# Shorter windows for the indirect transfers of a graph network kernel: scatters four deep, gathers of edge features six deep

## What is computed

```
h = relu(layernorm(x));  x += gated_network(h)   # 4 steps: msgs = (h W_k + b_k)[etype, src]; a = segment_sum(msgs, dst); GRU
h = relu(layernorm(x));  x += attention(h)       # softmax over the edges of a source, sum at the target
h = relu(layernorm(x));  x += segment_sum(h[src], dst)
h = relu(layernorm(x));  x += MLP(sum, max, mean of edge_attr over the edges of each src)
```

## Time and profile before

| | us |
|---|---|
| runs | 8828.69, 8854.78, 8858.06 |
| median | 8854.78 |
| profiled execution | 8876.89 |
| its span | 8875.0 |

### The profile page before, as it was taken

The page is one execution under the profiler, slowest core; times in us unless marked ns, Lnnn a source line. Parts: engine busy times, 40 slices in busy tenths (PEclk is TensorE's granted clock), DMA queues, the critical chain, the costliest instruction groups (busy, mean ns, idle before and its releaser), DMA issues. The chain is left out here.

```text
span 8875.0 us, 66244 instructions
## 1 busy us (share of the span) xinstructions
PE 4613.8 (52%) x21729; PEld 2818.2 (32%) x21729; DVE 4824.9 (54%) x9853; ACT 4454.6 (50%) x2943; POOL 3692.8 (42%) x3327
## 2 busy tenths in 40 slices
PE   0110001311113777676385555757839668788866
PEld 0100001100001333333274444546728556211135
DVE  9963346200002777776374333745629446888863
ACT  0000000200002999997385445647929668688855
POOL 0067773677775000000467444274865753000041
PEclk9555555555555888888697777878969879555578
DMA  9710000300101777777296555767829656455566
GB/s 415 340 0 0 0 0 29 94 18 7 33 4 64 298 303 297 303 296 266 90 310 182 150 165 167 231 182 243 307 74 343 222 201 235 177 223 219 217 241 217
DMA packets 523231, 1589.94 MB, mean 179 GB/s; under 512 B 148178, under 2 KB 207929, under 8 KB 493190
## 3 DMA queue, kind: packets, MB, share of 16 engines
q1 hardware_dynamic: 329082, 1408.51, 44.1%
q10 hardware_dynamic: 88332, 146.04, 5.0%
q0 software_dynamic: 105472, 31.16, 2.7%
HBM read 1046.14 MB, written 539.23 MB: 179 GB/s over the span
## 5 line engine op out<-in xcount | busy, mean ns | idle before, releaser
L1016 ACT ACTIVATE full<-ring 128x3136 fp32r<-128x3136 uint8 x731 | 1995.9, 2818 | 793.8 <-remote 469.6
L858 PE MATMUL ps_all<-full,TR 128*128 128x448 f32 x8232 | 1864.9, 383 | 651.1 <-ACT full L1016 248.0
L623 POOL DMA_INDIRECT mat_d<-cT,idxT x1563 | 1660.2, 1062 | 945.0 <-issue 485.2
L666 POOL DMA_INDIRECT two<-in_edge_attr,eid x1029 | 1183.2, 1150 | 1858.4 <-DMA csum_d<-two 1379.0
L858 PEld LDWEIGHTS ps_all<-full,TR 128*128 128x128 f32 x8232 | 1583.3, 196 | 929.5 <-issue 463.1
L809 PE MATMUL ps_all<-ring,T 128*64 128x448 f16 x8232 | 1159.5, 408 | 1377.3 <-issue 993.6
L1030 ACT ACTIVATE ring<-ring 128x3136 uint16<-128x3136 uint8 x197 | 553.4, 2809 | 1268.6 <-remote 1141.5
L809 PEld LDWEIGHTS ps_all<-ring,T 128*64 128x64 bf16 x8232 | 556.0, 124 | 1979.1 <-issue 1409.8
L1469 DVE CAST full<-ring 128x1568 fp32r<-128x1568 uint8 x487 | 478.5, 983 | 966.6 <-remote 451.9
L761 PE MATMUL ps_all<-ident,two 128*128 128x128 f32 x448 | 109.1, 424 | 1275.2 <-DVE two L1174 1113.2
L666 POOL DMA_INDIRECT ring<-in_edge_attr,eid x539 | 608.5, 1129 | 164.3 <-issue 164.3
(11 more groups left out here) (419 smaller groups left out, 6139.2 us busy)
## 6 DMA issues: line engine op xcount, KB each, us to landing
ring<-mat_d SPq DMA_DIRECT2D x784, 784.0 KB
mat_d<-ring SPq DMA_DIRECT2D x98, 1568.0 KB, 39.8
csum_d<-two SPq DMA_DIRECT2D x192, 784.0 KB
two<-csum_d SPq DMA_DIRECT2D x32, 3136.0 KB, 10.2
base_d<-two SPq DMA_DIRECT2D x49, 1568.0 KB
TR<-two_d SPq DMA_DIRECT2D x282, 256.0 KB
C<-csum_d SPq DMA_DIRECT2D x17, 3136.0 KB, 10.2
C<-base_d SPq DMA_DIRECT2D x49, 800.0 KB
```

The source lines that it names most:

```text
L623: pool.indirect_dma_start(mat_d, bass.IndirectOffsetOnAxis(idxT[:, col:col + 1], 0), cT[:, col:col + 1], None).then_inc(s_sc[g % 8], 16)
L666: pool.indirect_dma_start(slab[n % SLABS][:, c, 0:FA], None, attr, bass.IndirectOffsetOnAxis(eid[:, at:at + 1], 0)).then_inc(s_at[n % SLAB ...
L858: mm = pe.matmul(accs[:, j, 0:GW], parts.bitcast(F32R), full[:, m % WIDES, j * GW:(j + 1) * GW].bitcast(F32R), start=first, stop=True, ski ...
L1016: act.activation(to, own, ACT.Copy).then_inc(s_ha, 1)
```

## The change

`FETCHES = 6` and `AFLOAT = 4` are new. The scatters count on 4 semaphores in turn, one for each scatter instead of one for each group, and scatter k waits until scatter k - 4 has landed. `s_done` is raised ahead of the fifth scatter of the next group instead of the ninth. Gather `at` counts on semaphore `at % 6` and waits until gather `at - 6` has landed, across the slabs. VectorE waits for all six semaphores ahead of a scan.

```diff
+FETCHES = 6
+AFLOAT = 4
...
-            s_sc = dma_sems(*(t + f"scattered{k}" for k in range(8)))
+            s_sc = dma_sems(*(t + f"scattered{k}" for k in range(AFLOAT)))
...
-            s_at = dma_sems(*(t + f"slab{k}" for k in range(SLABS)))
+            s_at = dma_sems(*(t + f"fetched{k}" for k in range(FETCHES)))
...
-                    if a == GC // 2 and g:
-                        pool.wait_ge(s_sc[(g - 1) % 8], 16 * GC * ((g - 1) // 8 + 1))
+                    if k >= AFLOAT:
+                        pool.wait_ge(s_sc[k % AFLOAT], 16 * (k // AFLOAT))
+                    if a == AFLOAT and g:
                         pool.sem_inc(s_done, 1)
                     col = a * P + g
                     pool.indirect_dma_start(mat_d, bass.IndirectOffsetOnAxis(idxT[:, col:col + 1], 0),
-                                            cT[:, col:col + 1], None).then_inc(s_sc[g % 8], 16)
+                                            cT[:, col:col + 1], None).then_inc(s_sc[k % AFLOAT], 16)
...
-                last = NGC - 1
-                pool.wait_ge(s_sc[last % 8], sum(16 * (min(NCOL, (x + 1) * GC) - x * GC) for x in range(last % 8, NGC, 8)))
+                for k in range(AFLOAT):
+                    pool.wait_ge(s_sc[k], 16 * ((NCOL - 1 - k) // AFLOAT + 1))
...
+                        if at >= FETCHES:
+                            pool.wait_ge(s_at[at % FETCHES], 16 * (at // FETCHES))
                         pool.indirect_dma_start(slab[n % SLABS][:, c, 0:FA], None, attr,
-                                                bass.IndirectOffsetOnAxis(eid[:, at:at + 1], 0)).then_inc(s_at[n % SLABS], 16)
+                                                bass.IndirectOffsetOnAxis(eid[:, at:at + 1], 0)).then_inc(s_at[at % FETCHES], 16)
...
-                        dve.wait_ge(s_at[n % SLABS], 16 * SLAB * (n // SLABS + 1))
+                        for k in range(FETCHES):
+                            dve.wait_ge(s_at[k], 16 * (((n + 1) * SLAB - 1 - k) // FETCHES + 1))
```

More of the change, by code:

```diff
@@ L67 @@
 FIRST = 25
+FETCHES = 6
+AFLOAT = 4
 QW = 1568
 NQ = NP // QW
+assert NCOL % GC > AFLOAT or NCOL % GC == 0
 assert LP * LC == E and LC <= SW and COLS % 512 == 0 and NP * COLS <= TRASH and ALL < MARK
```

## The result

| | before, us | changed, us |
|---|---|---|
| median of four runs | 8844.66 (8828.69 to 8858.06) | 7643.63 (7601.50 to 7676.55) |
| profiled execution, its span | 8875.0 | 7599.4 |

The ratio is 0.866, with a 95% interval of 0.860 to 0.872: 1201 us less, where 45 us more was forecast. The two spans differ by 1275.6 us.

A forecast was written before the change was run, and what follows sets the result against it. The scatters' last part was taken to bound step 0, and slabs without slack the steps. Scatters 4 us plus gathers 41 us made 45 us on the median 8854.8: 8900 us forecast, range 8650 to 9035 us.

The forecast's parts named there:

- the slow regime gives way: Rival: the windows may break TensorE's crawl beside GpSimd's transfers; 8665 to 8783 us, or about 7760 at most; chance 0.25.
- 2 or 3 us of GpSimd's time: Right after the scatters restart, 1598.5 to 1604 us: the window of four binds and two or three us are lost.
- a calm stretch: Gathers, 6280 to 6300 us: 12 transfers landed while 14 were made, two or three in the air, six allowed.
- Rows 16: Stretches compared: 56 matmuls in 132 us at 1.42 us a transfer, 501 in 130 us at 1.53 us.
- Part 1: Scatters of the build: a wait on each, free when met at once, binding only at a few late places; 4 us.
- The upper bound of 125 us: Scatters: all 890 after the restart go from the faster to the slower pace, 0.14 us more each.
- Part 2: Gathers of steps 1 to 3: window of six makes slabs 3, 13 and 17 late, surfacing at 4, 14, 19; 41 us.
- One for one: VectorE's 41.3 us of added waits for late slabs pass in full to TensorE and the end; taken as 41 us.
- the 117 us that the prediction gave one: Steps: time one slow stretch of TensorE gives back if its crawl goes; two give 235 us.
- The Trainium skill's figure: Fixed cost of about 2 us plus bytes per transfer; no gather in the air for six places, sum nothing, 8855 us.

The follow-up runs named there:

- the run with eight: Kernel before with a wait on each scatter for the one eight ahead, gathers as before: 8893 us against 8895 us.
- the run with five: Changed kernel with five scatters afloat instead of four: 8611 us against the kernel before's 8777 us; on the chip without the crawl 6845 us, ratio 1.031.
- the run with the pause in the gathers: Changed kernel, every fourth gather also waiting for the one right before it: 8013 us, ratio 1.208, without the crawl; 8262 us on a chip with it.

## Why the prediction was wrong

**The sign and the size.** 8900 us was forecast, with 0.25 on faster; it came out at 7644 us. What came true is the rival *the slow regime gives way*, whose upper end was 1144 us for the contraction of step 0. Its span shrank by 1119 us.

**The step that failed** is the sentence against that rival: in the crawl the transfers land at once, so the new waits are met at once. It is true of the crawl, and the run with eight and the end of the run with five show it. But the windows act before the crawl is there. At 1598 us the kernel starts free, and in the first microseconds 5 scatters are made while 3 land. I priced this at 2 or 3 us of GpSimd's time and did not ask what the pause does to TensorE: 94 matmuls in the next 10 us in place of 7. From there the window goes on binding, 182 times, since a free TensorE makes the landings late. One freed start isn't enough: with five afloat TensorE also did 94 matmuls in those 10 us, and fell into the crawl by 1800 us. I read the counts of a calm stretch as what the changed kernel would meet, while the calm was itself made by TensorE's crawl.

**What the rows had.** Rows 16 show GpSimd at 1.42 us beside the crawl and at 1.53 us beside a free TensorE. I took this as a sign that the stream alone isn't the cause. Read as a threshold of pace it says what the runs found over long stretches: 1.25 to 1.42 us crawls, 1.63 and 1.72 us is free, and at 1.45 us the free running held for some 200 us and then fell. It doesn't hold for short ones: from 4875 to 4900 us the changed kernel makes 19 gathers, 1.32 us each, and TensorE does 106 matmuls beside them.

**Part 1, 4 us for the scatters.** GpSimd waited 246 us and its last scatter came 220 us later. The upper bound of 125 us was too low, for it took the pace from unwaited rows. On the chips with the crawl this cost next to nothing: ScalarE waited for the matrix 4 times, 9.9 us in all. On the chip without it, with the same four afloat (the run with the pause in the gathers), ScalarE waited 315.6 us, and the scatters bound step 0.

**Part 2, 41 us for the gathers.** The mechanism was right and the sizes were mixed: slab 4 waits 16.33 us (15.1 predicted), slab 14 20.45 us (29.7), slab 19 12.95 us (17.6). The sum of VectorE's waits is 241.9 us and not 104, since slabs 3, 8 to 10, 13 and 15 to 18 are late too; by my reading their slack had come from the crawl. And the end didn't follow: the steps are 148 us shorter. One for one from VectorE's waits to the end holds where there is no crawl (116 us of waits, 130 us of time), at almost three times the 41 us. Beside the crawl it is outweighed, for three of the eight slow stretches are gone. At the 117 us that the prediction gave one, that is 351 us less, and with the 180 us that VectorE waits longer 171 us, by estimate, for the 148 measured.

**The Trainium skill's figure.** The Trainium skill (DMA: Bandwidth & Descriptors, section Anatomy of one DMA, SWDGE path) gives such a transfer a fixed cost of some 2 us: by it no window would have bound. In the crawl the trace comes near it: 14 transfers landed in 20 us while 14 to 16 were made, about two in the air, which at a pace of 1.3 us is 2.6 us by estimate. Beside busy DMA engines it does not: the changed kernel's window of four bound 182 times, and the scatter started at 1600.32 us had not landed 9 us later. There the measurement decides.

## What to carry to other kernels

Before a wait is priced by the present counts of landings, ask whether the present state of the other engines is made by the very stream that the wait slows. Where an engine's matmuls per 250 us fall to a sixteenth beside another engine's transfers and nothing in its own waits says why, first try to thin that stream: here a scatter every 1.6 us instead of every 1.3 us was worth 1100 us. And time such a change on more than one chip, for on one of the four chips of the experiments this crawl did not exist, and windows and pauses at the scatters made the kernel 3 to 8% slower, partly by the gathers' window that two of these runs also had.

## What the runs showed of the hardware

- Beside long rows of GpSimd's indirect transfers of 128 elements, made every 1.25 to 1.32 us, TensorE's instructions were completed one in 1.40 us, in five of the six groups of runs. With one memset between the transfers, at 1.42 us, it was one in 0.70 us. At 1.63 and 1.72 us TensorE did its full count of over 1400 matmuls in 250 us. At the place looked at, VectorE and ScalarE had no such delay (0.04 and 0.06 us). Why is open.
- One program on chips of the same kind took 6636 us on one and, by medians, 8777 to 8941 us on three others. What differs between the chips is open.
- TensorE free and TensorE in the crawl are both possible with the same instructions. In the kernel before, the crawl began some 12 us after GpSimd resumed its transfers at 1589.6 us; with five afloat, the slide took about 100 us. It ended some 25 us after the last scatter.
- An instruction of GpSimd that waits for a landed transfer has the same gap of 0.30 us ahead of it as one without a wait.
